# Null-key scores of the first cross-attention: eight products for all heads and a move with the identity, in place of one-column products

## The chip, the cores and the metric

The kernel runs on one core of a Trainium2 chip. The metric is device time in microseconds (us) of one execution: 468.68 us, the median of three runs (468.66 to 470.43). The core's engines are called PE (matrix products; PEld is its weight load, which the trace lists apart), DVE (vector), ACT (scalar), POOL (GpSimd) and SP (which only issues transfers). Each has its own instruction stream, runs it in order, and waits for the others on semaphores.

## The reference

Six blocks follow one another on a small latent array `x` (2 batches, 64 queries, 256 features): cross-attention, self-attention, a feed-forward layer with experts, a second cross-attention, a state-space block with a memory, and a second expert layer. The change touches the first block only, and in it the score of one extra key, the null key:

```python
q = _split_heads(x @ Wq) * scale              # 2 batches, 16 heads, 64 queries, 64 features
k, v = split(context @ Wkv)                   # 1024 keys a batch
k = concatenate((nk, k), axis=-2)             # nk = null_kv[0], the same 64 numbers for every head
v = concatenate((nv, v), axis=-2)
sim = einsum('bhid,bhjd->bhij', q, k)         # column 0: q . nk
attn = softmax(sim)
out = layernorm(einsum(attn, v) @ Wout)
```

So the null key needs 2 x 16 x 64 = 2048 dot products of length 64.

## The kernel before, in words

Heads go in pairs: a pair's 2 x 64 features fill the 128 partitions. There are 8 pairs and 2 batches, so 16 steps, r = 0 to 15 (`ROWT`). `QF` (in the tile `work`) holds the scaled queries turned, features on the partitions: `QF[:, j, :]` is pair j, 128 features by 128 tokens (batch 0, then batch 1), in plain fp32. Keys are never formed. `query_keys(j)` (L1523) multiplies the queries of pair j with the key weights, 8 products with 64 rows of weights each; ACT and DVE split what comes out into a high part (L673; L672 keeps the second batch raw) and a low part (L1017), and `sim(r)` (L1546) multiplies the split queries with the split context, 24 products of 512 columns, into one of two pairs of banks. A score tile has 128 partitions: queries of the first head of the pair, then of the second.

In the trace a product of plain fp32 operands is two records of each kind: "x64" at L1634 is 32 products.

For each step, `softmax0` runs on two engines in turn: DVE takes the row maximum (L1036), takes the larger of it and the null score and negates it (L1044); ACT exponentiates (L712, and L714 for the null score); DVE adds and inverts (L1050, L1051); ACT scales (L717). PE then turns the probabilities (L1563, `turn_probs`), ACT keeps the high part (L693) and DVE the low one (L1024). Every two steps `attend(g)` (L1590) multiplies them with the split context, 96 products of 256 columns. Its first call stands between `sim(3)` and `turn_probs(2)`.

The context comes in 16 chunks. ACT makes the high part of a chunk (L662), DVE the low part (L1007, semaphore `ctx_lo`). Chunks 4 to 7 are what the first `attend` reads; the table `SPLIT_BEHIND` places them on ACT and DVE behind steps 0, 1 and 2. The first `attend` waits for `ctx_lo` to reach 8. POOL issues the transfers of chunks 4 to 15 (L541) and waits for the buffer of each to be free.

The null scores: at r = 0, between `query_keys(3)` and `query_keys(4)`, PE runs 32 products (L1634), one for each step and head of the pair: the weights are 64 features by 64 tokens, the moving operand is one column of 64 numbers (`nk`, in `cols`), and the result goes to column n of bank 2 (partitions 0 to 63, first head) or bank 3 (64 to 127, second head). DVE copies both halves to `null_s` (L1041, L1042) before its first L1044. ACT waits for the second copy (`null_sb`), and so does `sim(1)`, which writes over banks 2 and 3.

The order of the work is the order in which the code of each engine is written. There is no planner at this place.

Of the kernel before, what the change touches and what calls it, by code (L numbers as in the profile page):

```python
# [219 lines left out]
def cut(base, at, *free):  # L220
# [5 lines left out]
    if len(free) == 1:  # L226
# [5 lines left out]

ONCE = {
    "tensor_made": [
        "null_ps", "out0_ps", "kA_ps", "qA_ps", "vA_ps", "qTA_ps", "kTA_ps", "simA_ps", "ptA_ps", "outA_ps", "gh_ps", "g_ps",
        "q1_ps", "k1_ps", "v1_ps", "rb0_ps", "rb1_ps", "o1T1_ps", "o1T0_ps", "out1_ps", "dt_ps", "cums_ps", "decay0_ps", "decay1_ps",
        "conv45_ps", "xs0_ps", "G_ps", "xs1_ps", "z_ps", "ym0_ps", "ym1_ps", "ssq_ps", "y_tok_ps", "sc_ps", "pq_ps", "scT_ps", "km_ps", "vmT_ps",
        "rank_ps", "lg_ps", "vm_ps", "vg_ps", "pmT_ps", "gate_ps", "ret_ps", "route_ps", "maskT_ps"],
# [2 lines left out]
        "dtl", "cums", "ex0_ready", "ex1_ready", "th45", "z_tanh", "ysq0_ready", "ysq1_ready", "sct", "pq_sb", "km_sb", "vmT_sb",  # L241
        "vm_sb", "pm_exp", "vg_sb", "pmT_sb", "gate_tanh", "hn_hi", "maskT_sb", "rz"],
    "vector_made": [
        "null_sb", "nv_ready", "kn_ready", "simA_max", "probsA", "hm_ready", "gT_lo", "sums0_ready", "sums1_ready", "o1_ready1", "o1_ready0", 
        "dtn_ready", "xp_sb", "dtA_ready", "xc0", "xc45", "xc1", "M0_ready", "M1_ready", "ya0_ready", "ya1_ready", "scz", "scb_ready",
        "cmp_ready", "tie_ready", "lmax", "pm_ready", "hn_lo", "mask_ready", "rneg"],
}
# [2 lines left out]
def perceiver_kernel(nc, x_in, ctx_in, ctxT_in, units_in, const_in, cols_in, vecs_in, rows_in, gate_in, out):  # L250
    with ExitStack() as stack:
# [96 lines left out]
        zs = cut(small, 12, 2)  # L348
        stat = cut(small, 16, ROWT, 2)
        null_s = cut(small, 48, B * PAIRS)  # L350
        negm = cut(small, 64, B * PAIRS)
        rinv0, w_null = cut(small, 80, ROWT), cut(small, 96, ROWT)
        ssq, rqk = cut(small, 112, 8), cut(small, 120, 8)
# [177 lines left out]
        @block.gpsimd  # L531
        def _(pool):
            def load_chunk(n):

                before = [m for m in range(n) if STAGE[m] == STAGE[n]]
                if before:
                    pool.wait_ge(ev("ctx_lo"), before[-1] + 1)
                if STAGE[n] == 5 and not before:

                    pool.wait_ge(ev("qp_ps"), PAIRS)  # L540
                pool.dma_start(stage_of(n), chunk_src(n)).then_inc(chunk_in(n)[0], 16)  # L541

            def keep_w(part, p):
                if part == 0:
                    u = SPLIT[p // 2]
                    pool.wait_ge(ev(f"place{PLACE[u]}"), LANDED[u])
                    pool.wait_ge(ev(slot_free(p)[0]), slot_free(p)[1])
                    pool.tensor_copy(w_slot(0, p), half_in(p)).then_inc(ev(hi_done(p)[0]), 1)
                else:
                    lo, hi = lo_parts(p)["gpsimd"]  # L550
                    pool.wait_ge(ev(hi_done(p)[0]), hi_done(p)[1])
                    pool.tensor_tensor(w_slot(1, p)[:, lo:hi], half_in(p)[:, lo:hi], f32(w_slot(0, p)[:, lo:hi]),  # L552
                                       ALU.subtract).then_inc(ev("lo_by_gpsimd"), 1)

            pool.wait_ge(ev("const_in"), 16)
            for n in range(N_RSQRT):

                pool.wait_ge(ev("var_ready"), n + 1)
                src, dst, wide = {RSQRT_K: (ssq[:, 0:HA], rqk[:, 0:HA], HA), RSQRT_Q: (ssq[:, HA:], rqk[:, HA:], HA),
                                  RSQRT_PAIR: (ve2, rstd2, 2)}.get(n, (ve, rstd, 1))  # L560
                pool.tensor_tensor(dst, src, c_("neghalf").to_broadcast([P, wide]), ALU.pow)\  # L561
                    .then_inc(ev("rstd_ready"), 1)
                if n == 0:
                    pool.dma_start(cols[:, :], cols_in).then_inc(ev("cols_in"), 16)
                    for k in range(4, CHUNKS):
                        load_chunk(k)
                        if k == 7:
                            pool.dma_start(vecs[:, :], vecs_in.partition_broadcast(P)).then_inc(ev("vecs_in"), 16)
                            pool.dma_start(gatew, gate_in).then_inc(ev("gatew_in"), 16)

                    pool.wait_ge(ev("ctx_lo"), CHUNKS)
                    pool.memset(rows_raw[0:96], 0.0).then_inc(ev("rows_zero"), 1)
                    pool.wait_ge(ev("rows_zero"), 1)
                    for at in BIAS_AT:
                        pool.dma_start(rows_raw[at:at + E + 1, :], rows_in[0:E + 1, :]).then_inc(ev("rows_in"), 16)
                    pool.wait_ge(ev("rows_in"), 16 * len(BIAS_AT))
                    pool.tensor_copy(BR[0:96, 0:NROWS], rows_raw[0:96]).then_inc(ev("rows_hi"), 1)
                    pool.wait_ge(ev("rows_hi"), 1)
                    lows = BR[32:64, 0:NROWS]
                    pool.tensor_tensor(lows, rows_raw[32:64], f32(lows), ALU.subtract).then_inc(ev("rows_split"), 1)  # L580
                    pool.wait_ge(ev("rows_split"), 1)
                if n == 2:

                    pool.memset(G3, 0.0).then_inc(ev("g3_zero"), 1)
                if n == 8:

                    pool.memset(M3, 0.0).then_inc(ev("m3_zero"), 1)
                if n == 5:
                    for p in range(SLOTS, MOE0):
                        keep_w(1, p)  # L590
                if n == 6:

                    for m in range(4):
                        pool.memset(probs1[:, m, NCTX + NQ * (1 - m % 2):NCTX + NQ * (2 - m % 2)], 0.0)\
                            .then_inc(ev("pads_zero"), 1)
                    for p in range(MOE0, MOE0 + SLOTS):
                        keep_w(0, p)
                        keep_w(1, p)

                    pool.wait_ge(ev("rows2_in"), 4 * 16)  # L600
                    for n, (raw, (lo, hi)) in enumerate(((work, BIAS1), (xn, BIAS2))):
                        for m, at in enumerate(BIAS_AT[0:2]):
                            pool.tensor_copy(BR[at:at + E, lo:hi], raw[at:at + E, 0:hi - lo]).then_inc(ev("rows2_hi"), 1)
                            pool.wait_ge(ev("rows2_hi"), 2 * n + m + 1)
                        lows = BR[at:at + E, lo:hi]
                        pool.tensor_tensor(lows, raw[at:at + E, 0:hi - lo], f32(lows), ALU.subtract)\
                            .then_inc(ev("rows2_split"), 1)
                        pool.wait_ge(ev("rows2_split"), n + 1)

                    pool.wait_ge(ev(f"place{PLACE['mb2']}"), LANDED["mb2"])  # L610
                    wo = unit("mb2")[:, KT * DIN:].rearrange("p (k n) -> p k n", k=XST)
                    pool.tensor_tensor(wo, wo, bc(p_("gnorm_w"), 2, DIM), ALU.mult).then_inc(ev("wo_scaled"), 1)
                if n == 7:

                    pool.memset(XP[:, :, :, 0:TAPS - 1], 0.0).then_inc(ev("xp_zero"), 1)
                if n == N_RSQRT - 1:
                    for p in range(MOE0 + SLOTS, 2 * len(SPLIT)):
                        keep_w(1, p)
# [325 lines left out]
        def _(dve):  # L944
# [89 lines left out]
            def softmax0(r):  # L1034
                dve.wait_ge(ev("sim_done"), r + 1)
                step(dve.tensor_reduce(mx[:, r % 2:r % 2 + 1], W[r % 2][:, :], AX_X, ALU.max))  # L1036
                if r == 0:
                    for j in (2, 3):
                        keep_q_lo(0, j)
                    dve.wait_ge(*made("null_ps"))  # L1040
                    dve.tensor_copy(null_s[0:NQ], bank(2)[0:NQ, 0:ROWT])  # L1041
                    dve.tensor_copy(null_s[NQ:P], bank(3)[NQ:P, 0:ROWT]).then_inc(*tick("null_sb"))  # L1042
                    dve.wait_ge(*made("null_sb"))
# [415 lines left out]
        def _(pe):  # L1459
# [161 lines left out]
            for r in range(ROWT + 1):  # L1621
                if r < ROWT:
                    sim(r)
                if r == 0:
                    for j in (2, 3):
                        query_keys(j)
                    pe.wait_ge(ev("cols_in"), 16)
                    pe.wait_ge(ev("ql_sb"), 2)
                    pe.wait_ge(ev("q_raw"), 2)
                    for n in range(ROWT):  # L1630
                        b, j = n // PAIRS, n % PAIRS
                        for hh in range(2):
                            rows = slice(hh * DH0, (hh + 1) * DH0)
                            mm = pe.matmul(bank(2 + hh)[rows, n:n + 1], QF[rows, j, b * NQ:(b + 1) * NQ], p_("nk")[rows],  # L1634
                                           start=True, stop=True)
                    mm.then_inc(*tick("null_ps"))
                    for j in (4, 5):
                        query_keys(j)
                if 1 <= r <= 2:
                    query_keys(5 + r)  # L1640
                if r % 2 == 1 and r >= 3:
                    attend((r - 3) // 2)
                if r % 2 == 0 and r >= 4:
                    project_heads(r // 2 - 2)
                if r >= 1:
                    turn_probs(r - 1)
# [611 lines left out]
```

## Time and profile before

| | us |
|---|---|
| median of three runs | 468.68 |
| lowest and highest run | 468.66, 470.43 |
| span of the profiled execution | 467.3 |
| PE busy | 449.3 (96%) |
| DVE, ACT, POOL busy | 256.2, 240.2, 123.5 |
| first cross-attention's scores and values, until PE's last L1590 | 13.49 to about 232 |

All times in the trace count from the first instruction of the profiled execution. Only its span is shown; the median of the runs is 1.4 us above it, for what lies around the first and the last instruction. The page's chain of work that ended last goes over PE for 76% of the span. An engine's idle time costs something only where somebody waits for it.

### The profile page before, as it was taken

The numbers are of one execution on the slowest core, as the hardware profiler recorded it, in microseconds if no ns is written. First come the engines' busy times: TensorE is split into PE (matmuls) and PEld (weight loads), VectorE is DVE, ScalarE is ACT, GpSimd is POOL, SyncE is SP. The second block draws the span as 40 slices with busy tenths as digits, with TensorE's granted clock in tenths as the row PEclk, the third lists the DMA queues.
The fourth block names the chain that finished last, engine by engine and source line by source line (L and its number), as shares of the span: only waits on it lengthen the run. The fifth ranks groups of instructions, "written<-read, shape, count | busy, mean of one in ns | idle before, by whom it ended". The sixth has DMA issues, their size and how long they took to land.

```text
span 467.3 us, 8504 instructions
## 1 busy us (share of the span) xinstructions
PE 449.3 (96%) x3500; PEld 385.6 (83%) x3500; DVE 256.2 (55%) x455; ACT 240.2 (51%) x439; POOL 123.5 (26%) x113
## 2 busy tenths in 40 slices
PE   8999999999999999999987999999999999999997
PEld 7887989989897989899966677998666779778797
DVE  2656223245426232232045788985567765469996
ACT  2577334264445343242113777762788764347872
POOL 1110000002000500000021277966920000019795
PEclk9999999999999999999999999999999999999999
DMA  8925400005200020000039999998000039264000
GB/s 281 412 96 194 180 2 1 1 0 183 89 0 1 13 90 1 1 1 1 1 121 426 362 294 337 420 389 361 2 1 1 2 119 418 96 269 181 0 1 13
DMA packets 13191, 62.65 MB, mean 134 GB/s; under 512 B 1365, under 2 KB 3813, under 8 KB 7392
## 3 DMA queue, kind: packets, MB, share of 16 engines
q1 hardware_dynamic: 11072, 54.31, 30.8%
q0 software_dynamic: 2080, 7.80, 4.7%
q8 instruction: 28, 0.46, 0.4%
q14 instruction: 11, 0.09, 0.1%
HBM read 61.97 MB, written 0.13 MB: 133 GB/s over the span
## 4 chain that ended last, share of the span: by engine, by line
PE 76%; DVE 6%; ACT 5%; DMA 5%; POOL 3%; issue 3%; SPq 0%; DVEq 0%; ACTq 0%; POOLq 0%
PE W L1590 20%; PE W L1546 15%; PE W L1749 7%; PE W L1830 4%; DMA ctxmem<-units_dram 4%; PE W L1884 4%; PE W L1929 3%; PE W L1563 3%; POOL w_lo L552 3%; PE W L1947 2%; PE W L1612 2%; PE W L1469 2%; DMA fixed<-units_dram 1%; PE W L1871 1%; PE W L1498 1%
## 5 line engine op out<-in xcount | busy, mean ns | idle before, releaser
L1590 PE MATMUL W<-probs_turned_hi,ctx_split_hi 128*128 128x256 f32 x256 | 72.8, 285 | 2.6 <-issue 2.5
L1590 PE MATMUL W<-probs_turned_hi,ctx_split_lo 128*128 128x256 f32 x256 | 72.4, 283 | 0.0
L1590 PE MATMUL W<-probs_turned_lo,ctx_split_hi 128*128 128x256 f32 x256 | 72.4, 283 | 0.0
L1024 DVE TENSOR_TENSOR probs_turned_lo<-W,probs_turned_hi 128x512 fp32r<-128x512 f32 x32 | 20.6, 686 | 64.9 <-ACT probs_turned_hi L693 64.9
L1590 PEld LDWEIGHTS W<-probs_turned_hi,ctx_split_hi 128*128 128x128 f32 x256 | 49.1, 192 | 3.8 <-issue 3.3
L561 POOL TENSOR_TENSOR small<-small,const 128x1 f32<-128x1 f32 (+2 forms) x10 | 7.0, 697 | 163.4 <-DVE small L1097 75.3
L1590 PEld LDWEIGHTS W<-probs_turned_lo,ctx_split_hi 128*128 128x128 f32 x256 | 49.1, 192 | 0.2
L1590 PEld LDWEIGHTS W<-probs_turned_hi,ctx_split_lo 128*128 128x128 f32 x256 | 49.1, 192 | 0.0
L712 ACT ACTIVATE pbuf<-W,small 128x1024 f32<-128x1024 f32 x16 | 17.9, 1116 | 59.6 <-DVE small L1044 59.6
L552 POOL TENSOR_TENSOR w_lo<-arena,w_hi 128x320 fp32r<-128x320 f32 x30 | 41.3, 1390 | 26.1 <-ACT w_hi L634 25.6
L552 POOL TENSOR_TENSOR w_lo<-ctxmem,w_hi 128x320 fp32r<-128x320 f32 (+1 forms) x30 | 46.3, 1568 | 5.1 <-ACT w_hi L634 4.6
L987 DVE TENSOR_TENSOR w_lo<-arena,w_hi 128x704 fp32r<-128x704 f32 (+1 forms) x34 | 43.7, 1318 | 6.2 <-ACT w_hi L634 5.9
L1830 PE MATMUL W<-w_hi,acts 128*128 128x256 f32 x240 | 44.4, 287 | 0.0
L1546 PE MATMUL W<-ctx_turned_hi,q_keys_hi 128*128 128x512 f32 x128 | 41.1, 402 | 0.5 <-DVE q_keys_lo L1017 0.5
L634 ACT CAST w_hi<-arena 128x1024 fp32r<-128x1024 f32 x34 | 35.4, 1050 | 8.7 <-PE W L1749 4.1
L1546 PE MATMUL W<-ctx_turned_lo,q_keys_hi 128*128 128x512 f32 x128 | 39.7, 391 | 0.0
L1546 PE MATMUL W<-ctx_turned_hi,q_keys_lo 128*128 128x512 f32 x128 | 39.5, 390 | 0.0
L1830 PEld LDWEIGHTS W<-w_hi,acts 128*128 128x128 f32 x240 | 38.4, 190 | 0.2
L704 ACT COPY scr<-W 128x256 f32<-128x256 f32 x32 | 11.8, 368 | 48.9 <-PE W L1590 48.9
L987 DVE TENSOR_TENSOR w_lo<-ctxmem,w_hi 128x704 fp32r<-128x704 f32 x26 | 33.9, 1344 | 2.1 <-ACT w_hi L634 1.7
L1830 PE MATMUL W<-w_lo,acts 128*128 128x256 f32 x120 | 33.9, 282 | 0.0
L1749 PE MATMUL W<-w_hi,acts 128*128 128x512 f32 x104 | 33.5, 398 | 0.1
(403 smaller groups left out, 907.6 us busy)
## 6 DMA issues: line engine op xcount, KB each, us to landing
arena<-units_dram SPq DMA_DIRECT2D x22, 1024.0 KB, 11.5
ctxmem<-units_dram SPq DMA_DIRECT2D x16, 1024.0 KB, 15.2
fixed<-units_dram SPq DMA_DIRECT2D x6, 1024.0 KB, 6.1
pbuf<-ctx_dram POOLq DMA_DIRECT2D x4, 512.0 KB, 6.3
ctxmem<-ctxT_dram SPq DMA_DIRECT2D x8, 256.0 KB, 11.8
ctxmem<-ctx_dram SPq DMA_DIRECT2D x2, 1024.0 KB, 14.6
scr<-ctx_dram POOLq DMA_DIRECT2D x3, 512.0 KB, 4.2
vecs<-vectors_dram POOLq DMA_DIRECT2D x1, 1040.0 KB, 7.6
```

The costliest lines, as they stand in the source:

```text
L552: pool.tensor_tensor(w_slot(1, p)[:, lo:hi], half_in(p)[:, lo:hi], f32(w_slot(0, p)[:, lo:hi]), ALU.subtract).then_inc(ev("lo_by_gpsimd"), 1)
L634: act.copy(w_slot(0, p), half_in(p)).then_inc(ev(hi_done(p)[0]), 1)
L712: act.activation(probs0[:, r % 2, :], W[r % 2][:, :], ACT.Exp, bias=negm[:, r:r + 1], accum_out=stat[:, r, 1:2]).then_inc(ev("exp_done"), 1)
L987: dve.tensor_tensor(w_slot(1, p)[:, lo:hi], half_in(p)[:, lo:hi], f32(w_slot(0, p)[:, lo:hi]), ALU.subtract).then_inc(ev("lo_by_vector"), 1)
L1024: dve.tensor_tensor(PT[1][at], bank(4 + c).rearrange("p (t m) -> p t m", t=4), f32(PT[0][at]), ALU.subtract).then_inc(ev("pl_sb"), 1)
L1546: mm = pe.matmul(W[r % 2][:, kh * 512:(kh + 1) * 512], QP[a][:, c, j, :], CXT[z][:, c, kh * 512:(kh + 1) * 512], start=(c == 0 and n == 0) ...
L1563: mm = pe.transpose(bank(4 + c)[:, t * P:(t + 1) * P], probs0[:, r % 2, (4 * c + t) * P:(4 * c + t + 1) * P], ident)
L1590: mm = pe.matmul(ps, CXN[a][:, t, c * P:(c + 1) * P], PT[z][:, t, :], start=(t == 0 and n == 0), stop=(t == KEYT - 1 and n == 2))
L1749: mm = pe.matmul(bank(4 + hf), XS[a][:, e, k, :], w_slot(z, p)[:, hf * 512:(hf + 1) * 512], start=u == "m1e0" and k == 0 and n == 0, stop= ...
L1830: mm = pe.matmul(bank(n % (E + 1) % 4)[:, 0:DIM], UTS[a][:, t, :], w_slot(z, p)[:, (t % 4) * DIM:(t % 4 + 1) * DIM], start=(t == 0 and i = ...
L1884: mm = pe.matmul(W[r % 2][:, kh * 512:(kh + 1) * 512], QZ[at:at + 32, j // 2, b].rearrange("p h q -> p (h q)"), KEYS[at:at + 32, b, j // 2 ...
L1929: mm = pe.transpose(bank((4, 5, 7)[c])[:, t * P:(t + 1) * P], probs1[:, r % 4, (3 * c + t) * P:(3 * c + t + 1) * P], ident)
```

## The change

Since the null key is the same for every head, one product of a whole pair (128 features by 128 tokens as weights) with a matrix of two columns gives both heads' scores of all tokens of the pair. The two columns hold `nk` in partitions 0 to 63 and zeros below, and zeros above and `nk` below (`nk_heads`). POOL makes this matrix from `cols` between two of its transfers. Eight products then give the scores with tokens on the partitions. They have to go to another place (query of the first head, query of the second head on the partitions; batch and pair in the columns), and so DVE copies them to `null_q`, and PE moves them with four products whose weights are halves of the identity. `query_keys(4)` stands between the products and the moves.

```diff
+        null_q, nk_heads = cut(small, 256, PAIRS, 2), cut(small, 272, 2)
...
                     for k in range(4, CHUNKS):
                         load_chunk(k)
+                        if k == 5:
+                            pool.memset(nk_heads, 0.0).then_inc(ev("nk_zero"), 1)
+                            pool.wait_ge(ev("nk_zero"), 1)
+                            pool.wait_ge(ev("cols_in"), 16)
+                            for hh in range(2):
+                                rows = slice(hh * DH0, (hh + 1) * DH0)
+                                pool.tensor_copy(nk_heads[rows, hh:hh + 1], p_("nk")[rows]).then_inc(ev("nk_heads"), 1)
...
                 if r == 0:
-                    for j in (2, 3):
-                        keep_q_lo(0, j)
+                    keep_q_lo(0, 2)
+                    dve.wait_ge(*made("nullq_ps"))
+                    dve.tensor_copy(null_q, bank(2)[:, 0:ROWT].rearrange("p (j h) -> p j h", h=2))\
+                        .then_inc(*tick("null_q"))
+                    keep_q_lo(0, 3)
                     dve.wait_ge(*made("null_ps"))
...
-                    pe.wait_ge(ev("cols_in"), 16)
+                    pe.wait_ge(ev("nk_heads"), 2)
                     pe.wait_ge(ev("ql_sb"), 2)
                     pe.wait_ge(ev("q_raw"), 2)
-                    for n in range(ROWT):
-                        b, j = n // PAIRS, n % PAIRS
-                        for hh in range(2):
-                            rows = slice(hh * DH0, (hh + 1) * DH0)
-                            mm = pe.matmul(bank(2 + hh)[rows, n:n + 1], QF[rows, j, b * NQ:(b + 1) * NQ], p_("nk")[rows],
-                                           start=True, stop=True)
+                    for j in range(PAIRS):
+                        mm = pe.matmul(bank(2)[:, 2 * j:2 * j + 2], QF[:, j, :], nk_heads, start=True, stop=True)
+                    mm.then_inc(*tick("nullq_ps"))
+                    query_keys(4)
+                    pe.wait_ge(*made("null_q"))
+                    for hh in range(2):
+                        rows = slice(hh * DH0, (hh + 1) * DH0)
+                        for b in range(B):
+                            mm = pe.matmul(bank(2 + hh)[rows, b * PAIRS:(b + 1) * PAIRS], ident[:, b * NQ:(b + 1) * NQ],
+                                           null_q[:, :, hh], start=True, stop=True)
                     mm.then_inc(*tick("null_ps"))
-                    for j in (4, 5):
-                        query_keys(j)
+                    query_keys(5)
```

On PE, at the end of step 0 of the kernel before. L1523 is `query_keys`, L1634 the null scores, L1546 `sim(1)`; the names after "waits" are semaphores.

```order
L1523 MATMUL W<-work,fixed 128x128 [waits q_raw,ql_sb]
L1523 MATMUL W<-work,fixed 128x128 x7
L1634 MATMUL W<-cols,work 64x1 [waits q_raw,ql_sb,cols_in]
L1634 MATMUL W<-cols,work 64x1 x31
L1523 MATMUL W<-work,fixed 128x128 [waits q_raw,ql_sb,place2]
L1523 MATMUL W<-work,fixed 128x128 x7
L1523 MATMUL W<-work,fixed 128x128 [waits q_raw,ql_sb]
L1523 MATMUL W<-work,fixed 128x128 x7
L1546 MATMUL W<-ctx_turned_hi,q_keys_hi 128x512 [waits vector_made,ql_sb]
```

The same place on PE in the changed kernel, where `query_keys` is L1535, the products are L1643, the moves L1650 and `sim` is L1558.

```order
L1535 MATMUL W<-work,fixed 128x128 [waits q_raw,ql_sb]
L1535 MATMUL W<-work,fixed 128x128 x7
L1643 MATMUL W<-small,work 128x2 [waits q_raw,ql_sb,nk_heads]
L1643 MATMUL W<-small,work 128x2 x7
L1535 MATMUL W<-work,fixed 128x128 [waits q_raw,ql_sb,place2]
L1535 MATMUL W<-work,fixed 128x128 x7
L1650 MATMUL W<-small,const 64x8 [waits vector_made]
L1650 MATMUL W<-small,const 64x8 x3
L1535 MATMUL W<-work,fixed 128x128 [waits q_raw,ql_sb]
L1535 MATMUL W<-work,fixed 128x128 x7
L1558 MATMUL W<-ctx_turned_hi,q_keys_hi 128x512 [waits vector_made,ql_sb]
```

The last of the null score's instructions on PE has moved behind `query_keys(4)`, and only `query_keys(5)` is left between it and `sim(1)`.

On DVE, the first softmax step of the kernel before: L1036 is the row maximum, L1017 the low parts of the queries, L1041 and L1042 the copies to `null_s`, L1044 the negated maximum.

```order
L1036 TENSOR_REDUCE small<-W 128x1 [waits sim_done]
L1017 TENSOR_TENSOR q_keys_lo<-W,q_keys_hi 128x4x128 [waits qh_sb,vector_step]
L1017 TENSOR_TENSOR q_keys_lo<-W,q_keys_hi 128x4x128 [waits qh_sb]
L1041 COPY small<-W 64x16 [waits tensor_made]
L1042 COPY small<-W 64x16
L1044 TENSOR_SCALAR small<-small 128x1 [waits vector_made]
```

The same place on DVE in the changed kernel, in the same order of lines (L1045, L1026, then the new copy L1049).

```order
L1045 TENSOR_REDUCE small<-W 128x1 [waits sim_done]
L1026 TENSOR_TENSOR q_keys_lo<-W,q_keys_hi 128x4x128 [waits qh_sb,vector_step]
L1049 COPY small<-W 128x16 [waits tensor_made]
L1026 TENSOR_TENSOR q_keys_lo<-W,q_keys_hi 128x4x128 [waits qh_sb]
L1053 COPY small<-W 64x16 [waits tensor_made]
L1054 COPY small<-W 64x16
L1056 TENSOR_SCALAR small<-small 128x1 [waits vector_made]
```

A third copy, with a wait for PE of its own, now stands between the two low parts.

## Rows read from the trace of the kernel before

**Rows 1.** Chain that ended last, in order of time: start us, us, what.

```profile
19.36 1.99 PE W L1523 x32
21.35 1.98 PE W L1634 x64
23.35 0.17 DVE small L1041
...
23.75 0.23 DVE small L1044
...
24.06 1.20 ACT pbuf L712 x2
...
28.96 0.96 ACT ctx_split_hi L662
...
30.01 2.36 DVE ctx_split_lo L1007 x2
...
47.57 11.74 PE W L1590 x96
```

**Rows 2.** Timeline around the first attend: start us, us, engine line op [idle before].

```profile
46.25 1.22 DVE L1007 TENSOR_TENSOR ctx_split_lo<-scr,ctx_split_hi 128x1024 fp32r<-128x1024 f32 x1
...
47.57 0.36 PE L1590 MATMUL W<-probs_turned_hi,ctx_split_hi 128*128 128x256 f32 x1 [1.43 <-issue]
```

**Rows 3.** Timeline from the null scores to the first exponential, all engines.

```profile
21.27 1.94 PEld L1634 LDWEIGHTS W<-cols,work 64*64 64x64 f32 x64
...
21.68 0.69 DVE L1017 TENSOR_TENSOR q_keys_lo<-W,q_keys_hi 128x512 fp32r<-128x512 f32 x1 [1.06 <-ACT q_keys_hi L673]
...
22.58 0.69 DVE L1017 TENSOR_TENSOR q_keys_lo<-W,q_keys_hi 128x512 fp32r<-128x512 f32 x1 [0.21 <-ACT q_keys_hi L673]
23.23 1.86 PEld L1523 LDWEIGHTS W<-work,fixed 64*128 64x128 f32 x32
...
24.06 1.11 ACT L712 ACTIVATE pbuf<-W,small 128x1024 f32<-128x1024 f32 x1 [1.51 <-DVE small L1044]
...
25.22 0.30 PEld L1546 LDWEIGHTS W<-ctx_turned_hi,q_keys_hi 128*128 128x128 f32 x2
```

**Rows 4.** Timeline of weight loads elsewhere, weights rows*columns after the names.

```profile
30.89 0.97 PEld L1523 LDWEIGHTS W<-work,fixed 64*128 64x128 f32 x16 [0.35 <-issue]
...
31.98 0.53 PEld L1563 LDWEIGHTS W<-const,pbuf 128*128 128x128 f32 x5
```

**Rows 5.** The same, a product of eight columns and what follows it.

```profile
411.29 0.52 PEld L2136 LDWEIGHTS W<-cols,xT 128*128 128x128 f32 x4 [0.70 <-ACT xT L627]
411.73 0.19 PEld L1469 LDWEIGHTS W<-const 128*128 128x128 f32 x1
```

**Rows 6.** The same, weights of 128 rows and 64 columns.

```profile
65.82 1.01 PEld L1612 LDWEIGHTS W<-scr,fixed 128*64 128x64 f32 x32
66.90 0.53 PEld L1563 LDWEIGHTS W<-const,pbuf 128*128 128x128 f32 x5
```

**Rows 7.** Timeline of POOL and of the chunk that it loads there.

```profile
4.08 0.56 POOL L561 TENSOR_TENSOR small<-small,const 128x1 f32<-128x1 f32 x1 [3.63 <-DMA const<-constants_dram]
...
15.21 1.42 POOL L541 DMA_DIRECT2D pbuf<-ctx_dram  x2 [3.41 <-DVE ctx_turned_lo L1007]
```

**Rows 8.** Timeline: POOL's next transfer, ACT's first use of chunk 6.

```profile
31.53 0.72 POOL L541 DMA_DIRECT2D scr<-ctx_dram  x1 [14.90 <-DVE ctx_split_lo L1007]
...
37.61 1.06 ACT L662 CAST ctx_split_hi<-pbuf 128x1024 fp32r<-128x1024 f32 x1
```

**Rows 9.** Landing of the columns' transfer: DMA issues, KB, us to landing.

```profile
cols<-columns_dram POOLq DMA_DIRECT2D x1, 36.5 KB, 6.0
```

**Rows 10.** Stretches: us, busy PE, PEld, DVE, ACT, POOL, granted clock, DMA, GB/s.

```profile
46.10:47.60 1.50, 0.07 (x2) 0.06 (x1) 1.42 (x3) 0.12 (x1) 0.00 (x0) 1.00 0.01 5
325.20:328.60 3.40, 3.40 (x16) 3.10 (x15) 2.01 (x4) 1.81 (x5) 3.32 (x3) 0.50 0.11 46
```

**Rows 11.** Chain that ended last, a later wait of PE.

```profile
150.79 1.10 issue
```

More of the change, by code:

```diff
@@ L234 @@
     "tensor_made": [
-        "null_ps", "out0_ps", "kA_ps", "qA_ps", "vA_ps", "qTA_ps", "kTA_ps", "simA_ps", "ptA_ps", "outA_ps", "gh_ps", "g_ps",
+        "nullq_ps", "null_ps", "out0_ps", "kA_ps", "qA_ps", "vA_ps", "qTA_ps", "kTA_ps", "simA_ps", "ptA_ps", "outA_ps", "gh_ps", "g_ps",
         "q1_ps", "k1_ps", "v1_ps", "rb0_ps", "rb1_ps", "o1T1_ps", "o1T0_ps", "out1_ps", "dt_ps", "cums_ps", "decay0_ps", "decay1_ps",
@@ L243 @@
     "vector_made": [
-        "null_sb", "nv_ready", "kn_ready", "simA_max", "probsA", "hm_ready", "gT_lo", "sums0_ready", "sums1_ready", "o1_ready1", "o1_ready0",
+        "null_q", "null_sb", "nv_ready", "kn_ready", "simA_max", "probsA", "hm_ready", "gT_lo", "sums0_ready", "sums1_ready", "o1_ready1", "o1_ready0",
         "dtn_ready", "xp_sb", "dtA_ready", "xc0", "xc45", "xc1", "M0_ready", "M1_ready", "ya0_ready", "ya1_ready", "scz", "scb_ready",
```

## The prediction, made before the changed kernel was run

> **What bounds the kernel now.** I read the page first: PE is busy for 96% of the span, so the first guess is that a shorter train on PE is time won. The chain of work that ended last corrects this for the stretch in which the change lies [rows 1]. It runs over PE up to the null scores (L1523, L1634), but at 23.35 us it leaves PE: DVE copies the null scores, negates the maximum (23.75), ACT exponentiates (24.06), splits chunks of the context (28.96), DVE makes their low parts (30.01) and takes the next maximum, and so on in turns between ACT and DVE until chunk 7's low part. Only at 47.57 us, with the first `attend`, does the chain come back to PE. The timeline shows the joint [rows 2]: DVE's low part of chunk 7 ends at 46.25 + 1.22 = 47.47, PE starts `attend` at 47.57, and it has stood idle for 1.43 us before it. The view files that wait under "issue", but the semaphore is `ctx_lo`, and the times fit within 0.1 us. From there on PE is the chain for most of the span.
>
> So between 23.3 and 47.6 us PE has 1.43 us to give, and what sets the end is the moment at which `null_s` is written. Each us by which the null scores come later goes down the ACT and DVE chain, for ACT's and DVE's steps there follow each other with gaps of under 0.1 us: ACT's chunk ends at 28.96 + 0.96 = 29.92, DVE's low parts start at 30.01. What PE itself wins or loses there is only seen beyond those 1.43 us.
>
> **What the change removes, adds and moves.** *The products.* Before, 64 weight loads of 64x64 run from 21.27 to the next load at 23.23, 1.96 us or 31 ns each [rows 3]. Now there are 8 products, 16 loads, with full 128x128 weights and 2 columns. The nearest row is a product of 128x128 fp32 weights with 8 columns, L2136: four loads from 411.29 to the next one at 411.73, 110 ns each [rows 5]. That gives 16 x 0.110 = 1.76 us, only 0.2 us less than the 32 small products. The other bound is the pace of `query_keys`, whose weights have the same 128 columns but 64 rows: 32 loads in 25.22 - 23.23 = 1.99 us, 62 ns each [rows 3], or 16 x 0.062 = 0.99 us. I take 110 ns, since that row has the full shape.
>
> The Trainium skill (TensorE: Matmul & The Clock Gate, LDWEIGHTS) says that a load's time goes by the number of its columns and not by its rows: 107 ns for 128 columns, 53 ns for 64. By that rule alone the 64 old loads would be 3.4 us and the 16 new ones 1.7 us, a gain of 1.7 us. The trace agrees on the full shape (110 ns), but not on the old loads, at 31 ns: they alternate between two quarters of the array and evidently load side by side. The rule leaves that out, and it is why the saving by count isn't there.
>
> *Changes of shape.* From 64-row to 128-row weights there is a small gap: 16 loads of L1523 from 30.89 at 62 ns end at 31.88, L1563 starts at 31.98 [rows 4]. That is 0 to 0.1 us, twice.
>
> *The move.* Four products are 8 loads of 128 rows and 64 columns. L1612 has that shape: 32 loads from 65.82 to the next load at 66.90, 34 ns each with the gap at their end. But its products alternate between the two column halves of the array [rows 6]. In the new code the first four loads go to one half and the last four to the other, so half the full load's 110 ns, 55 ns, is the other bound. 8 of them: 0.27 to 0.44 us; I take 0.36. From the last load's slot to DVE's copy it takes 23.35 - 23.23 = 0.12 us [rows 1, 3].
>
> *The order.* `query_keys(4)` now stands ahead of the moves: 16 loads at 62 ns, 0.99 us. Before, it stood behind `null_ps`, where nobody waited for it. This is the largest term.
>
> *The sum on PE.* 21.27 + 1.76 = 23.03, with half a gap 23.1; `query_keys(4)` to 24.1; a gap and the moves to 24.5; DVE's first copy at 24.65, against 23.35. The null scores come 1.3 us later. The ends are 24.4 (no gaps, short moves: 1.05 us) and 24.95 (both gaps, long moves: 1.6 us). With the 62 ns pace the products end at 22.26. `query_keys(4)` needs the low part of pair 2, which DVE has ready at 22.37 [rows 3], so it runs from 22.45 to 23.45, and the copy is at about 23.85: 0.5 us later.
>
> *DVE.* The new copy is 0.17 us, like L1041. It waits for the products, at about 23.25, and the low part of pair 3 is queued behind it (0.69 us, before at 22.58 to 23.27). It now ends at 23.25 + 0.17 + 0.69 = 24.1. `query_keys(5)` wants it at 24.5 and the copies of `null_s` at 24.65, so both are covered by PE's own train; the cover is 0.4 us, and were it gone, what is missing would be added to the 1.3.
>
> *`sim(1)`.* `query_keys(5)` ends at 24.5 + 0.99 = 25.5 and `null_s` is safe at 25.0, so `sim(1)` starts at about 25.5 in place of 25.22, 0.3 us later. That is inside PE's 1.43 us and costs nothing. PE then waits 1.43 + 1.3 - 0.3 = 2.4 us before `attend`.
>
> *POOL.* After the issue of chunk 5 at 15.21 (0.7 us) come one memset and two one-column copies. At 0.56 us each, as for the 128x1 operation of L561 [rows 7], or at nothing, they end between 15.9 and 17.6. The columns have landed at 4.58 + 6.0 = 10.6 [rows 9]. PE wants the matrix at 21.27, with 3.7 us to spare. Queued behind is the transfer of chunk 6, which goes from 15.9 to at most 17.6; ACT first reads it at 37.61, and POOL's next transfer waits until 31.53 anyway [rows 8]. Nothing.
>
> *The sum.* ACT's first exponential and all behind it are 1.3 us later, `attend` starts at 48.9 in place of 47.57, and PE, which bounds from there, carries it to the end. The profiled execution would span 467.3 + 1.3 = 468.6; the median of the runs lies 1.4 us above the span, so 470.0 us.
>
> **Rivals.** *A: the products go at 62 ns.* For it: the same weights are read there at this pace with 64 rows. Against: rows 5. The delay is 0.5 us: 469.2.
>
> *B: PE's own train decides, not slower.* If the 1.43 us before `attend` were PE's own delay in fetching its instructions, as the word "issue" could be read, the start of `attend` would follow PE. At 62 ns a product load and 34 ns a move's, PE's null work is 0.99 + 0.27 = 1.26 us in place of 1.96, and the kernel gains 0.7 us: 468.0. At 110 ns it is 0.3 us slower, 469.0. Against it stand the 0.1 us between DVE's end and PE's start, and the semaphore. It decides as soon as `attend` moves with PE and not with L1007.
>
> *C: the delay is absorbed further on.* At 150 us PE waits once more for chunks, 1.1 us [rows 11]. Those are split behind steps that come after `attend`, and so move with it. If transfers that don't move set a later stage, the time stays at 468.7.
>
> *D: PE's clock falls.* The granted clock is full in the wait before `attend` [rows 10], and it is at half, 1.2 GHz, once in the span, for 3.4 us from 325.2, in which PE is busy throughout. One such stretch in the `attend` stage, which PE bounds, costs half its length, 1.7 us: 470.0 + 1.7 = 471.7. For it: PE's wait grows from 1.43 to 2.4 us, the longest in the kernel, and the three runs before already spread over 1.8 us. Against: no wait of the trace brought it about, and the one fall came without any.
>
> The Trainium skill (TensorE: Matmul & The Clock Gate, the HAM clock gate) has the clock halved when PE has been idle and restored by activity; it would make D likelier the longer the wait. The trace bears out neither side, since its longest wait passed at full clock.
>
> **How the numbers follow.** The forecast holds with 0.58, A with 0.10, B with 0.04, C with 0.06, D with 0.20, anything else with 0.02. The time is 470.0 us. The range of 468.7 to 471.9 leaves out B's gain and D's upper edge. What a measurement of this kernel can tell from no change is about 0.5%, 2.3 us: 466.3 and 471.0 are the bounds. The forecast, A, B and C lie within them, D above. I give 0.01 to faster, 0.77 to the same and 0.22 to slower.
>
> **What the changed profile would show.** Right: 16 loads of the products in about 1.8 us; the first `null_s` copy at 24.4 to 24.95; ACT's first exponential at 25.4; `attend` at 48.9 with some 2.4 us of idle PE before it and DVE's low part of chunk 7 ending just before; the same length from there to the end. A shows in loads 62 ns apart. B would show `attend` away from the end of L1007. D would show half clock between 46 and 60 us. The forecast is wrong if the first exponential is no later than 24.6, if `attend` starts with it unmoved, or if the end doesn't keep the shift.

## The result, and the profile after

| kernel | runs | median us | lowest, highest |
|---|---|---|---|
| before | 4 | 469.44 | 468.66, 470.43 |
| changed | 4 | 475.75 | 471.06, 477.88 |

The ratio is 1.012, with a 95% interval of 1.007 to 1.0171: slower by 1.2%, clear of the interval, where the forecast was 470.0 in a range up to 471.9. Both kernels scatter more than the three runs first shown let one think. In all, the changed kernel was run 28 times (median 473.2, mean 473.5) and the kernel before 117 times (469.3 and 469.8), 113 of them in the later sets. So the usual loss is 3.7 to 3.9 us, 0.8%, and the first four runs were on the high side of it. Two later sets, each on a chip of its own, gave 1.0058 [1.0024, 1.0092] and 1.0065 [1.0035, 1.0095]. The medians below are of all runs of a kernel, while the ratios leave out runs that are over 1.5% above its fastest one.

The page of the changed kernel has the busy time of each engine, and the clock granted to PE in 40 slices of the span.

```profile
span 472.3 us, 8429 instructions
PE 453.4 (96%) x3460; PEld 389.2 (82%) x3460; DVE 256.2 (54%) x456; ACT 240.6 (51%) x439; POOL 125.8 (27%) x116
...
PEclk9999899999999999999999999999899999999999
```

Two slices are below 9. On the page of the kernel before none is, since its one fall lies across the border of two slices. The chain of the changed kernel, in order of time (start us, us, what), answers to [rows 1]. L1535 is `query_keys`, L1643 the products, L1650 the moves, L1053 the copy to `null_s`, L721 the exponential, L1016 chunks' low parts, L1602 `attend`.

```profile
14.85 5.85 PE W L1558 x24
20.70 1.99 PE W L1535 x32
22.68 1.88 PE W L1643 x16
24.56 1.09 PE W L1535 x16
25.65 0.37 PE W L1650 x8
26.03 0.03 issue
26.05 0.17 DVE small L1053
...
26.76 1.21 ACT pbuf L721 x2
...
32.71 2.36 DVE ctx_split_lo L1016 x2
...
50.26 13.24 PE W L1602 x96
63.50 0.87 PE W L1575 x8
...
77.67 11.52 PE W L1602 x96
```

The first 96 products of `attend` took 13.24 us, the next 11.52; before, the first took 11.74. The timeline around the null scores (as [rows 3]) has the new pieces one by one; L1049 is DVE's new copy to `null_q`.

```profile
22.61 1.86 PEld L1643 LDWEIGHTS W<-small,work 128*128 128x128 f32 x16
...
24.49 0.97 PEld L1535 LDWEIGHTS W<-work,fixed 64*128 64x128 f32 x16
...
24.60 0.18 DVE L1049 COPY small<-W 128x16 f32<-128x16 f32 x1 [0.89 <-PE W L1643]
24.69 0.68 DVE L1026 TENSOR_TENSOR q_keys_lo<-W,q_keys_hi 128x512 fp32r<-128x512 f32 x1
25.58 0.32 PEld L1650 LDWEIGHTS W<-small,const 128*64 128x64 f32 x8
...
25.92 0.97 PEld L1535 LDWEIGHTS W<-work,fixed 64*128 64x128 f32 x16
```

And the wait before `attend` (as [rows 2]):

```profile
48.93 1.23 DVE L1016 TENSOR_TENSOR ctx_split_lo<-scr,ctx_split_hi 128x1024 fp32r<-128x1024 f32 x1
...
50.26 0.36 PE L1602 MATMUL W<-probs_turned_hi,ctx_split_hi 128*128 128x256 f32 x1 [2.29 <-issue]
```

In stretches (us, busy PE, PEld, DVE, ACT, POOL, granted clock, DMA, GB/s), as [rows 10]: the wait, what follows it, and the fall in the second cross-attention that the kernel before has too, at 325 us.

```profile
47.31:50.72 3.41, 1.12 (x7) 0.69 (x7) 3.08 (x4) 1.59 (x3) 0.27 (x1) 1.00 0.01 2
50.72:54.13 3.41, 3.41 (x19) 3.41 (x18) 1.57 (x6) 2.13 (x4) 0.79 (x2) 0.50 0.66 234
330.61:334.03 3.42, 3.42 (x14) 2.78 (x13) 1.61 (x4) 1.64 (x5) 3.34 (x3) 0.50 0.01 2
```

From 0.46 us after the end of the wait PE ran at 1.2 GHz for 3.4 us. So the 5.05 us between the two profiled spans fall into four parts. I cut every profile at the same five starts: the first L1546 (sim 0), ACT's first exponential, the first L1590 (attend), PE's first product of the self-attention (239.94 in the kernel before), and its first of the second cross-attention (317.00). Between the last two lie the self-attention and the first expert layer. The last column is what remains of the span.

| profile | sim 0 | to exp | to attend | PE idle before it | to self-attention | to second cross-attention | rest |
|---|---|---|---|---|---|---|---|
| before | 13.49 | 10.57 | 23.51 | 1.43 | 192.37 | 77.06 | 150.30 |
| changed | 14.85 | 11.91 | 23.50 | 2.29 | 193.85 | 77.90 | 150.29 |

The null scores are 1.34 us later, the first block is 1.48 us longer from `attend` on, the stretch with the expert layer 0.84 us, and 1.36 us are there before anything that the change touches has run.

### The profile page after: what moved, and what is told of

The parts are those of the page before. It is cut to its first block, busy times and chain, and to the rows that moved or that the text cites. A ratio compares the mean times of both kernels' runs of the same rounds, so it can differ in the third digit from the quotient of the medians.

```text
span 472.3 us, 8429 instructions
## 1 busy us (share of the span) xinstructions
PE 453.4 (96%) x3460; PEld 389.2 (82%) x3460; DVE 256.2 (54%) x456; ACT 240.6 (51%) x439; POOL 125.8 (27%) x116
## 4 chain that ended last, share of the span: by engine, by line
PE 77%; DVE 6%; ACT 5%; POOL 5%; DMA 4%; issue 3%; SPq 0%; DVEq 0%; ACTq 0%; POOLq 0%
PE W L1602 20%; PE W L1558 15%; PE W L1764 7%; PE W L1845 4%; POOL w_lo L553 4%; PE W L1899 4%; PE W L1944 3%; DMA arena<-units_dram 3%; PE W L1575 3%; PE W L1962 2%; PE W L1624 2%; PE W L1481 2%; PE W L1510 1%; PE W L1535 1%; POOL small L562 1%
## 5 line engine op out<-in xcount | busy, mean ns | idle before, releaser
L1602 PE MATMUL W<-probs_turned_hi,ctx_split_hi 128*128 128x256 f32 x256 | 73.6, 287 | 3.4 <-issue 3.4
L1602 PE MATMUL W<-probs_turned_lo,ctx_split_hi 128*128 128x256 f32 x256 | 73.1, 286 | 0.0
L1602 PE MATMUL W<-probs_turned_hi,ctx_split_lo 128*128 128x256 f32 x256 | 73.1, 286 | 0.0
L1602 PEld LDWEIGHTS W<-probs_turned_hi,ctx_split_hi 128*128 128x128 f32 x256 | 49.8, 194 | 4.6 <-issue 4.2
L1602 PEld LDWEIGHTS W<-probs_turned_lo,ctx_split_hi 128*128 128x128 f32 x256 | 49.9, 195 | 0.2
L1602 PEld LDWEIGHTS W<-probs_turned_hi,ctx_split_lo 128*128 128x128 f32 x256 | 49.8, 195 | 0.0
L721 ACT ACTIVATE pbuf<-W,small 128x1024 f32<-128x1024 f32 x16 | 17.9, 1117 | 62.7 <-DVE small L1056 62.7
L1558 PE MATMUL W<-ctx_turned_hi,q_keys_hi 128*128 128x512 f32 x128 | 41.1, 402 | 0.5 <-DVE q_keys_lo L1026 0.5
L1558 PE MATMUL W<-ctx_turned_lo,q_keys_hi 128*128 128x512 f32 x128 | 39.7, 391 | 0.0
L1558 PE MATMUL W<-ctx_turned_hi,q_keys_lo 128*128 128x512 f32 x128 | 39.5, 390 | 0.0
## 6 DMA issues: line engine op xcount, KB each, us to landing
ctxmem<-ctxT_dram SPq DMA_DIRECT2D x8, 256.0 KB, 11.9
```

The source lines that it names most:

```text
L721: act.activation(probs0[:, r % 2, :], W[r % 2][:, :], ACT.Exp, bias=negm[:, r:r + 1], accum_out=stat[:, r, 1:2]).then_inc(ev("exp_done"), 1)
L1558: mm = pe.matmul(W[r % 2][:, kh * 512:(kh + 1) * 512], QP[a][:, c, j, :], CXT[z][:, c, kh * 512:(kh + 1) * 512], start=(c == 0 and n == 0) ...
L1602: mm = pe.matmul(ps, CXN[a][:, t, c * P:(c + 1) * P], PT[z][:, t, :], start=(t == 0 and n == 0), stop=(t == KEYT - 1 and n == 2))
```

## The experiments

Twelve experiments were run, in three sets, each set beside 31 to 35 runs of the kernel before. The number of half-clock stretches of a run is worked out from its mean granted clock c and its span s as (1 - c) s / 1.71, rounded to a whole number, since a stretch is 3.41 us at half. It says how many there were, and not where; for the place there is only the one profiled execution of each experiment. The kernel before has 0.50 of them in the mean of its 113 runs, the changed one 2.18 in 28, and none of the 28 had fewer than one.

**The kernel before again.**

> The kernel before, unchanged, profiled once more. The profiled pair differs by 5.05 us: 1.36 us are there before the first sim product already (14.85 against 13.49 us), 1.34 us come between it and ACT's first exponential, 1.7 us in the first attend, where the clock was at half for 3.4 us, and 0.6 us in the expert layer. If the 1.36 us are chance of the first transfers, the first L1546 starts anywhere from 13 to 15 us here, and the time of this kernel lies from 468.5 to 470.5. If the transfers were slower in the changed kernel because of it, this one starts at 13.5 again and stays under 469.

Measured 468.39 us (466.78 to 472.29), a little under the 468.5 to 470.5 expected, with 0.42 stretches and sim 0 at 14.10. In the profiles with the old POOL code the first product starts at 13.26 to 15.39 us, in those with the new code at 13.19 to 15.21. So the 1.36 us are chance; that it is the first transfers which scatter was not looked into.

**The changed kernel again, twice.**

> The changed kernel, unchanged. Theory 1 (later null scores, longer idle PE before the first attend, then clock at half in it): first exponential 13.3 us behind the start of the first sim product minus 1.4, that is 11.9 us behind it (10.6 before); PE idle 2.2 to 2.4 us before attend; clock at half in the attend stage; median 3 to 6 us over the kernel before. Rival 2 (chance of the first transfers): with more runs the medians lie 1.3 us apart. Rival 3 (the half clock has another cause than the wait): half clock in other places than right behind 50 us.

> The changed kernel once more, for where its stretches lie and for its median against the kernel before on another chip. Theory 1a: half clock right behind the wait before attend in this profile too, 2 to 2.5 stretches a run in the mean, 472 to 474 in the median against 469 to 469.5.

Measured 472.89 (469.92 to 476.23) and 473.66 (470.73 to 477.92), with 2.25 and 2.08 stretches. Both profiles have half clock from 50.1 and 50.5 us on, and another stretch at 255 and 300 us. Theory 1 held for the wait, but in each profile the other stretch lies elsewhere.

**The changed kernel with the wait filled.**

```diff
+                if g == 0:
+                    pe.wait_ge(ev("ql_sb"), PAIRS)
+                    pe.wait_ge(ev("q_raw"), PAIRS)
+                    stay_warm(7, 9)
                 pe.wait_ge(ev("pl_sb"), 4 * (g + 1))
```

> The changed kernel, with 9 dummy products of the identity (about 0.22 us each, 2.0 us) on PE in the wait before the first attend. They delay nothing that the wait doesn't cover. Theory 1: no half clock in the first attend, so 1.7 us or more less than the changed kernel in the median, 470 to 471.5, and a narrower spread. Rival 2: same as the changed kernel. Rival 3: the half clock stays, and so does the time.

Measured 471.72 us (469.19 to 477.55), ratio 1.0033 [0.9997, 1.0068], 1.08 stretches in place of 2.2. `attend` ran at full clock: 192.37 us to the self-attention. The median is 1.2 us below that of the changed kernel in the same set, where 1.7 or more was expected, and the means of the two, 472.8 and 473.0, can't be told apart. In the profile one stretch began 1.7 us behind the last load of the narrow products, the new ones with two moving columns, with `query_keys` and the moves in between (stretches, as above):

```profile
21.62:25.03 3.41, 3.41 (x44) 3.25 (x46) 1.59 (x4) 1.12 (x3) 0.00 (x0) 1.00 0.84 338
25.03:28.44 3.41, 3.41 (x20) 2.82 (x19) 0.76 (x5) 2.40 (x4) 0.00 (x0) 0.50 0.03 11
```

PE is listed as busy throughout before this fall. It slowed PE's train, so that the dummy products began late and ended behind DVE's last low part:

```profile
47.79 1.22 DVE L1016 TENSOR_TENSOR ctx_split_lo<-scr,ctx_split_hi 128x1024 fp32r<-128x1024 f32 x1
...
48.20 2.17 PE L1481 MATMUL W<-const 128*128 128x128 f32 x18
...
50.13 0.36 PE L1605 MATMUL W<-probs_turned_hi,ctx_split_hi 128*128 128x256 f32 x1
```

DVE ended at 49.01, 23.40 us behind the exponential as in the changed kernel, and `attend` started only at 50.13. So this fall cost the chain nothing, and the dummy products that it pushed back cost 1.0 us. The spread did not narrow: in this profile the stretch with the expert layer took 83.75 us in place of 77, with a wait of PE of 5.7 us in it.

**The kernel before, with nothing but a later null score.**

```diff
+                    step(dve.tensor_reduce(mx[:, 1:2], W[0][:, :], AX_X, ALU.max))
                     dve.wait_ge(*made("null_ps"))
```

> The kernel before with its 64 small loads as they were, and one more row maximum of 1.23 us on DVE ahead of the copies of the null scores, so that null_s comes about 1.3 us later, as in the changed kernel. Theory 1: the same as the changed kernel: attend 1.3 us later, PE idle 2.7 us before it, half clock behind it, 3 to 6 us over the kernel before. If the products or moves of the changed kernel were the cause in any other way than by the time of null_s (rival 3), it is 1.3 us slower than before and no more.

> The kernel before with the extra row maximum ahead of the copies of the null scores, once more, since the execution that was profiled the first time ran at 0.85 of the clock throughout. Theory 1: exponential 11.85 us behind the first sim product, attend 23.5 us behind that, 2.7 us of idle PE before attend, half clock right behind the wait (attend to the next layer 193.9 us in place of 192.4), mean number of half-clock stretches about 1.3 and median about 471. If the wait alone did not bring the fall about, full clock there and 0.5 stretches.

Measured 470.87 and 472.50 us (ratios 1.0032 [1.0002, 1.0063] and 1.0067 [1.0032, 1.0101]). One run of the first set, the profiled one, took 503.73 us at 0.84 of the clock and is left out of what follows. The other 23 runs had 1.5 stretches in the mean, and each had at least one. In time the first set alone, 1.5 us over the kernel before, fits the 1.3 us of rival 3 and not the 3 to 6 us of theory 1; the second is 3.3 us over. Together their mean is 2.4 us over that of the kernel before, uncertain by 0.9, where the later null scores and one fall would give 1.1 + 1.5 = 2.6. The second profile: the exponential 11.65 us behind sim 0, and then

```profile
47.45:50.86 3.41, 0.92 (x8) 0.82 (x8) 3.34 (x4) 1.26 (x2) 0.59 (x2) 1.00 0.01 2
50.86:54.27 3.41, 3.41 (x19) 3.41 (x18) 1.24 (x6) 2.45 (x4) 0.45 (x1) 0.50 0.79 274
```

PE idled for 2.49 us and the clock fell 0.79 us after it; 193.84 us to the self-attention. The old products with a late `null_s` bring about the same two losses as the change. Rival 3 is out as the main cause of the fall at this place.

**The same, with the wait filled.** Ten dummy products, the edit as above.

> The kernel before with the extra row maximum, and 10 dummy products (2.2 us) in the wait before attend. Theory 1: the chain's 1.3 us stay, the stretch behind the wait goes: 0.4 to 0.6 stretches, median 470.5, attend to the next layer 192.4 us. If the idle time has nothing to do with the clock: 1.3 stretches and 471, as without the dummies.

Measured 470.27 us (469.41 to 475.62), ratio 1.0019 [0.9987, 1.0051], 0.58 stretches. The same two stretches of this profile:

```profile
47.30:50.70 3.40, 3.15 (x25) 2.88 (x24) 2.78 (x4) 1.88 (x3) 0.00 (x0) 1.00 0.01 2
50.70:54.10 3.40, 3.40 (x30) 3.40 (x30) 1.81 (x6) 1.82 (x4) 1.05 (x2) 1.00 0.67 196
```

With PE kept busy until 0.25 us before `attend`, 30 products ran in the time of 19. The self-attention came after 192.36 us. The mean is 2.3 us below that of the same kernel without dummies in the same set, uncertain by 1.4. What is left is the chain's 1.1 us: `attend` still starts 23.48 us behind an exponential that is 11.66 us behind sim 0.

**128 moving columns in place of 2.**

```diff
-                            pool.memset(nk_heads, 0.0).then_inc(ev("nk_zero"), 1)
+                            pool.memset(hn[:, 0:P], 0.0).then_inc(ev("nk_zero"), 1)
...
-                        mm = pe.matmul(bank(2)[:, 2 * j:2 * j + 2], QF[:, j, :], nk_heads, start=True, stop=True)
+                        mm = pe.matmul(W[1][:, j * P:(j + 1) * P], QF[:, j, :], hn[:, 0:P], start=True, stop=True)
```

> The changed kernel with a moving matrix of 128 columns, of which 126 are zeros, in place of 2, for the eight products; the load of the weights sets their pace either way (114 ns a record with 128 columns at L1498, 117 ns with 2), so the null scores come within 0.1 us of the changed kernel's. Theory 1a (the changed kernel's clock falls for two reasons, the longer wait before attend and the narrow products at 21 to 25 us): one half-clock stretch a run less than the changed kernel has (from about 2.2 to 1.3 in the mean), never one at 25 us; 0 to 1.7 us faster, since a stretch at 25 us is partly hidden by PE's wait. Rival 4 (only the wait makes the clock fall): no change of the mean number of stretches and none of the time.

> The same with 128 columns, and the 9 dummy products in the wait before attend. Theory 1a: the mean number of half-clock stretches goes back to the kernel before's, about 0.4, and what is left is the later null score: 1.3 us over the kernel before, 470.3. Rival 4: as the changed kernel with dummies alone, 1.1 stretches and 471.7. If the later null score costs nothing by itself: as the kernel before, 469.

The products now write to 1024 columns of `W[1]` in place of 16 of bank 2, and DVE picks the two useful columns of each 128 out of them; that part of the edit is not shown. The first of the two experiments has this edit alone, the second the dummy products as well. The weight loads of the products, of the wide kernel:

```profile
22.99 1.86 PEld L1643 LDWEIGHTS W<-hn,work 128*128 128x128 f32 x16
```

The same 1.86 us: 64 times the columns are free here. Without dummies 472.96 us (469.42 to 474.40, 8 runs), ratio 1.0045 [1.0016, 1.0074], 1.38 stretches; with dummies 471.40 us (469.13 to 474.55, 12 runs), 1.0026 [1.0000, 1.0051], 0.58 stretches. The narrow products thus account for about 0.8 stretches (2.18 to 1.38, uncertain by 0.6) and, with dummies, for 0.5 (1.08 to 0.58, uncertain by 0.7). With dummies the stretches went where theory 1a had them, and the time stayed within 0.3 us of what rival 4 had, 471.7. So whether the narrow products account for time is less clear: the wide kernels' medians lie 0.3 us below the narrow one's with dummies and between 0.1 us above and 0.7 us below it without, for sets of 8 and 12 runs that spread over 5 us.

**`query_keys(4)` behind the moves.** The edit is the order alone.

> The changed kernel with query_keys(4) behind the moves in place of ahead of them, as in the kernel before. The forecast's largest term says that the 1.0 us of query_keys(4) delays the null scores: now PE waits some 0.35 us for DVE's null_q copy instead, and the first exponential comes 11.3 us behind the first sim product in place of 11.9 (10.6 in the kernel before). The wait before attend shrinks by 0.6 us less the 0.3 us by which PE is later. Time about 0.6 us under the changed kernel, perhaps with fewer half-clock stretches behind the wait. Rival 2: no difference.

Measured 469.97 us (468.44 to 473.92), 1.0013 [0.9987, 1.0038], 0.67 stretches: within noise of the kernel before, and 3.2 us under the changed kernel's 28 runs, where 0.6 us was expected. The exponential is 11.19 us behind sim 0, against 11.9; PE idled for 0.75 us before `attend`. In its profile the clock fell at 26.73, 2.1 us behind the last load of the narrow products. `sim(1)` took 6.73 us in place of 5.49 and held up DVE and ACT in their next steps (DVE's row maximum at 34.65 stood waiting for it), so `attend` came 24.39 us behind the exponential in place of 23.50, although PE still had idle time before it.

```profile
23.30:26.70 3.40, 3.13 (x45) 3.03 (x46) 1.83 (x6) 1.29 (x3) 0.00 (x0) 1.00 0.38 151
26.73:30.14 3.41, 3.41 (x18) 2.70 (x17) 0.34 (x3) 2.98 (x7) 0.00 (x0) 0.50 0.02 5
```

**Both mends.**

> Both mends of the changed kernel at once: query_keys(4) behind the moves, and 128 moving columns in place of 2. Theory 1a: exponential 11.3 us behind the first sim product, no fall at 25 us, and the wait before attend short (about 1.6 us), so 0.4 to 0.6 stretches and a median 0.7 us over the kernel before, 470. If it has 1 stretch or more and 471 or more, the narrow products were not what cost the clock at 25 us.

Measured 470.66 us (470.25 to 472.31), 1.0021 [0.9994, 1.0047], 0.42 stretches. The timeline of its PE and DVE:

```profile
23.31 0.17 DVE L1049 COPY small<-W 128x16 f32<-128x16 f32 x1 [0.99 <-PE W L1643]
...
23.54 0.32 PEld L1649 LDWEIGHTS W<-small,const 128*64 128x64 f32 x8 [0.46 <-DVE small L1049]
...
24.01 0.17 DVE L1053 COPY small<-W 64x16 f32<-64x16 f32 x1
```

The exponential is 11.25 us behind sim 0 and the wait before `attend` 1.41 us, with full clock behind it. Stretches are back at the number of the kernel before; the 0.7 us of the chain remain. Against the order alone this is 0.42 stretches in place of 0.67, which 12 runs each can't tell apart.

**The kernel before with its own wait filled.** Five dummy products.

> The kernel before with 5 dummy products of the identity (1.1 us) in its own wait of 1.43 us before attend. If the kernel before loses some of its runs' time to a fall of the clock at this wait, its mean number of half-clock stretches falls from 0.4 to under 0.2 and its median by up to 0.5 us. If its stretches lie elsewhere (the expert layers' waits), no change.

Measured 469.19 us (467.28 to 473.23), 0.9986 [0.9960, 1.0013], 0.33 stretches. A gain can't be told from none, and no version tried beats the kernel before.

**Waits of PE elsewhere.** The traces hold more waits than the one before `attend`. In the expert layer PE waits for DVE's low part of the weights, for a different time in each profile. Three of these waits, from the second rerun of the changed kernel, the wide kernel with dummies, and the first rerun of the changed kernel:

```profile
299.42 0.39 PE L1845 MATMUL W<-w_hi,acts 128*128 128x256 f32 x1 [1.81 <-DVE w_lo L996]
...
297.00 0.39 PE L1848 MATMUL W<-w_hi,acts 128*128 128x256 f32 x1 [2.33 <-DVE w_lo L996]
...
298.65 0.38 PE L1845 MATMUL W<-w_hi,acts 128*128 128x256 f32 x1 [1.45 <-DVE w_lo L996]
```

Behind the waits of 1.81 and 2.33 us the clock fell, at 299.69 and 298.38, and in the one of 5.7 us it fell while PE still stood. Behind the one of 1.45 us it did not. These waits are for weights and not for the null scores, so they bear out at a second place what theory 1 says of a long wait. But not every fall has a long wait ahead of it. The one that the kernel before has at 325.18 us comes out of a stretch in which PE is busy throughout, with products of 32 rows:

```profile
321.76:325.18 3.42, 3.42 (x40) 2.54 (x40) 2.27 (x5) 1.33 (x3) 3.34 (x3) 1.00 1.00 410
```

A fall stands behind these products in four of the 13 profiles (the one at 0.84 of the clock is left out). The falls at 253 to 255 us, in three profiles, come out of stretches in which PE is busy for 1.96 to 1.99 of 3.4 us, with no single wait over 0.7 us.

## Why the prediction was wrong, point by point

**Bound.** Right. `attend` moved with L1007 (now L1016), and the time from the exponential to it is 23.5 us in both kernels. Rival B is out.

**Products.** Right: 117 ns a load against 110, 1.88 us against 1.76. Rival A is out.

**Moves and order.** Right: 25.58 to 25.92, 0.34 us against 0.36; `query_keys(4)` 1.09 us with its gap against 0.99. Putting it back behind the moves took 0.7 us from the delay, a little less than its length, since PE then waits some 0.3 us for DVE's copy.

**The null scores.** Right: 1.34 us later (1.38 and 1.36 in the two further profiles, at the exponential) against 1.3. The sum's late end is off by itself: 23.03 + 0.1 + 0.99 + 0.1 + 0.44 + 0.12 is 24.78, or 1.4 us, not 24.95 and 1.6. DVE's low part of pair 3 ended at 25.37, ahead of PE's need at 25.92, so its cover held.

**PE's wait.** Right: 2.29 us against 2.4.

**POOL.** Right that nobody waits for the matrix: its two copies ran from 17.48 to 18.84 and PE wanted it at 22.6. Each took 0.68 us, more than the 0.56 that was its bound, and the memset 0.12. Whether the later transfers behind it cost anything further on is taken up under "The rest".

**Absorbed further on.** Wrong as a rival: from `attend` to the self-attention it is 192.35 to 192.37 us in every profile with full clock there.

**The clock.** This is the step that failed. The sum had the right wait of 2.4 us and put what it does to the clock at nothing; rival D, one fall, had 0.20, with the argument that no wait of the trace had brought a fall about. That the longest wait seen, 1.43 us, passed at full clock says nothing about one of 2.3. In the five profiles with 2.25 to 2.5 us of idle PE there (three of the changed kernel, the wide one, the late one) the clock fell 0.4 to 1.3 us after its end each time; in the eight with 1.43 us or less, or with the wait filled, it never did there. D's price was about right, 1.48 us for 1.7. Forecast and D together are 2.8 us, and would have been 471.5. That is still inside the range, so the one fall behind the wait is not the whole of the miss.

**What no rival had.** The changed kernel has 1.7 stretches a run more than the kernel before (2.18 against 0.50), and the fall behind the wait is one of them. The old products with a late `null_s` have 1.5, so that about 0.7 go with the new products, uncertain by 0.4. The full-shape products with two columns are a likely second occasion for a fall, at 25 to 27 us: it was seen in two of five profiles with such products and in none of the eight others, 1.7 and 2.1 us behind their last load. But both of the two are of edited kernels. None of the three profiles of the changed kernel itself has it; their second stretches lie at 255, 300 and 331 us. So that the narrow products bring falls is made likely by the counts and not shown, and why they would is open. With a filled or a short wait such a fall cost 1.0 and 0.9 us; behind the 2.3 us of the changed kernel it might cost less, which no profile shows.

**The rest.** The means differ by 3.7 us, of which 1.34 and 1.48 are shown. The other 0.9 us aren't settled. The difference of the means is itself uncertain by 0.9 us at 95%, worked out from the spread of the two sets. The extra stretches could hold it. So could the self-attention and expert layer: they took 77.0 to 79.4 us in the five profiles with the old POOL code and 77.8 to 83.8 in the eight with the new one. That the change makes PE wait longer there, by its place between two transfers of POOL, is a rival that no experiment tested. The further 2.3 us by which the first four runs' median lies above the 473.5 can be chance of four runs, since the later 24 don't repeat it.

**The range.** It was built on three runs with 1.8 us between them. The 113 later runs of the kernel before go from 466.8 to 477.2, eight in ten from 467.6 to 472.2, and their median is 0.6 us above the one I started from. Three runs show too little of such a scatter to set a range's end by.

## What to carry to other kernels

Fewer instructions are not a shorter train: 64 small loads that alternate between quarters of the array took 1.96 us, 16 full ones 1.88. If the result of a small step starts a chain on other engines, its delay counts in full there, and the longer wait that PE has at the chain's end can cost as much again in clock. 2 us of dummy products in the wait took that second half away where nothing else had slowed PE; where something had, they ran past the end of the wait and cost 1.0 us. Do not put work that nobody waits for between a result and its user.

## What the runs showed of the hardware

- Granted clock: all seven waits of PE of 1.81 to 2.5 us (five before `attend`, two in the expert layer) were followed by 3.4 us at 1.2 GHz, which began 0.3 to 1.4 us after the end of the wait, and in one of 5.7 us the clock fell while it lasted. Of 20 waits of 1.1 to 1.48 us none was.
- The clock also falls behind stretches in which PE is listed as busy all the time: in four profiles at 325 to 331 us, behind products of 32 rows, and in one at 25 us, out of a stretch with weight loads of full shape and two moving columns. With 128 moving columns the loads took as long, 1.86 us, and in three profiles the fall was not seen.
- fp32 loads: 117 ns for 128 rows and 128 columns; 42 ns for 128 rows and 64 columns when four loads in a row go to the same half of the columns, against 34 when the half changes with every product, that is every two loads.
- A 64x1 copy on POOL took 0.6 to 0.7 us, a 64x16 copy from the banks on DVE 0.17 us.
